# Cross-attention and expert feed-forward: rows of the feed-forward in 32 tiles of 256 and 9 of 128, with three buffers of raw weights

## The chip, the cores and the metric

The kernel runs on one core of one Trainium2 chip. The time is the device time of the whole program in microseconds; the median of three runs of the kernel before is 916.47 us (913.32 to 917.2). The profile is of one execution of its own.

## What is computed

x is (4, 1024, 256), float32. First a cross-attention with 16 heads of 64 over a context of 77 rows is added to x. Then each of the 4096 rows is normalised, scored against 9 experts, and the two best experts of each row are applied and added, weighted:

```
logits = x @ Wr                        # (4096, 9)
topk_w, topk_idx = top_k(softmax(logits), 2);  topk_w /= sum(topk_w)
hidden = silu(x @ Wg[e]) * (x @ Wu[e]) # 256 -> 704, for each expert e
out    = sum over the two experts of cw[t, e] * (hidden @ Wd[e])   # 704 -> 256
```

So 8192 pairs of row and expert go through the feed-forward, spread unevenly over 9 experts. Wg and Wu are 256 x 704 each, Wd is 704 x 256: 2.2 MB for one expert.

## The kernel before

The attention runs first, 32 steps of 128 rows, written out. In it GpSimd scatters each normalised row twice into expert_in in DRAM, once for each of its experts; each expert has a region there. The feed-forward then reads tiles of W = 256 rows that belong to one expert. Each expert's rows are rounded up to whole tiles, so NT is fixed at 40, the most that can be needed; tiles that are not needed are computed on blank rows all the same, and add into a blank part of the result. Three short tables that VectorE works out after the attention (tile_table: expert, first row and weight slot of a tile; fresh: whether its expert differs from the one before) tell which rows and weights a tile takes.

All products of the feed-forward are float32 made of three products of rounded parts: a value is split into "hi" (rounded by ScalarE) and "lo" (the rest, by VectorE), and hi*hi, hi*lo, lo*hi are accumulated (lines 248 to 250). This holds for the weights too: every tile splits its whole expert, six pieces (PIECES: four of 704 columns, one of 1280, one of 256), into wgt_hi and wgt_lo, two buffers of each. The raw weights have two buffers, wgt[0] and wgt[1], by the expert's parity.

One step of the feed-forward, tile j:
- TensorE (expert_step): gate and up products in three units (gate_up, 24, 24 and 18 matmuls of 256 columns; weights stationary, tokens moving, so the hidden rows come out turned as the down product needs them). After the second unit the tokens of tile j + 1 are transposed (tok_turn, line 1183, four transposes), then comes the down product of tile j - 1 (down, lines 248 to 250 and 1216, 34 matmuls), then the third unit.
- ScalarE: silu of a unit, then two pieces of wgt_hi for tile j + 1 (line 930), then the rounding of the hidden rows (946); after the second unit also the tokens of j + 1 (917) and the result of tile j - 1, scaled by the gate (res_move, 957).
- VectorE: the product of a unit (1572 to 1575), two pieces of wgt_lo (1564), the rest of the hidden rows (1583 to 1587); after the second unit the tokens' rest (1552).
- GpSimd: add_results (line 758) scatters the tile's result with addition, two DMAs, waits until they have landed, and then notes gate and row number of tile j + 2 (note, lines 749, 750).
- SyncE (step): waits until tile j - 1 is turned and noted, loads the tokens of tile j + 1 (line 542), loads expert, slot and flag of that tile into registers, and issues its weights (lines 526 to 535), three DMAs for gate and up, three for down, which do nothing where the flag is zero.

The waits that set the order of weight loads and tokens are these:

```python
sp.wait_ge(tok_turned, j)
sp.wait_ge(tok_noted, j)
load_tokens(j + 1, i)
sp.wait_ge(weights_split, j * len(PIECES) - (len(PIECES) - 2 * KT))   # then load_gate_up
sp.wait_ge(weights_split, j * len(PIECES))                            # then load_down
```

Steps 3 to 38 are a loop of two steps (Fori) on every engine; the others are written out. Before step 0 SyncE has loaded the weights of experts 0 and 1 during the end of the attention, blanks the end of each expert's region (store_tail), and loads the tokens of tiles 0 and 1.

## Time and profile before

| | us |
|---|---|
| median of 3 runs | 916.47 |
| profiled execution, its time | 915.46 |
| its span | 913.3 |
| TensorE matmul busy | 848.4 |
| VectorE busy | 694.3 |
| ScalarE busy | 650.1 |
| GpSimd busy | 395.9 |
| raw weights asked for in a tile's step | 3 + 3 DMAs, 40 times |

Times in a timeline are microseconds from the start of the span. A matmul's own duration overlaps that of the next one, so the distance between two starts is what a matmul costs. "x2" on a row is two instructions merged into one row. "SPq" is an instruction that issues a DMA on SyncE. The feed-forward runs from about 389 to the end.

### The profile page before, as it was taken

The numbers are of one execution on the slowest core, as the hardware profiler recorded it, in microseconds if no ns is written. First come the engines' busy times: TensorE is split into PE (matmuls) and PEld (weight loads), VectorE is DVE, ScalarE is ACT, GpSimd is POOL, SyncE is SP. The second block draws the span as 40 slices with busy tenths as digits, with TensorE's granted clock in tenths as the row PEclk, the third lists the DMA queues.
The fourth block names the chain that finished last, engine by engine and source line by source line (L and its number), as shares of the span: only waits on it lengthen the run. The fifth ranks groups of instructions, "written<-read, shape, count | busy, mean of one in ns | idle before, by whom it ended". The sixth has DMA issues, their size and how long they took to land.

```text
span 913.3 us, 21992 instructions
## 1 busy us (share of the span) xinstructions
PE 848.4 (93%) x6494; PEld 810.5 (89%) x6494; DVE 694.3 (76%) x1610; ACT 650.1 (71%) x2009; POOL 395.9 (43%) x536
## 2 busy tenths in 40 slices
PE   6998999999999997099999999999999999999993
PEld 5845999999999996099999999999999999999993
DVE  7577898888898877668777787678687786778771
ACT  3557898898888883267777777677677776777761
POOL 3020387787787676204433333332334333333432
PEclk9999999999999999599999999999999999999997
DMA  8054910400400217602225225444532255222222
GB/s 278 2 148 129 273 37 30 139 31 30 140 31 30 82 37 266 162 25 44 39 46 138 40 46 132 108 102 113 131 47 40 50 133 118 55 41 46 40 29 24
DMA packets 66697, 78.37 MB, mean 86 GB/s; under 512 B 7319, under 2 KB 58707, under 8 KB 66643
## 3 DMA queue, kind: packets, MB, share of 16 engines
q1 hardware_dynamic: 50963, 57.73, 21.5%
q0 software_dynamic: 14592, 18.95, 12.4%
q10 hardware_dynamic: 1088, 1.06, 0.5%
q8 instruction: 24, 0.39, 0.2%
q14 instruction: 30, 0.25, 0.1%
HBM read 113.66 MB, written 33.13 MB: 161 GB/s over the span
## 4 chain that ended last, share of the span: by engine, by line
PE 68%; DMA 12%; issue 7%; SPq 5%; DVE 4%; ACT 2%; POOL 1%; DVEq 0%; ACTq 0%; POOLq 0%
PE banks L248 20%; PE banks L249 19%; PE banks L250 19%; DMA wgt<-in_L_ffn_Wu 5%; PE banks L1116 4%; DMA result<-res,tok_id 3%; DMA valmat_dram<-val_st 2%; PE banks L1216 1%; PE banks L1183 1%; DVE hid_lo L1583 1%; SPq L478 1%; PE banks L1048 1%; POOL result L758 1%; PE banks L1072 1%; PE banks L1084 1%
## 5 line engine op out<-in xcount | busy, mean ns | idle before, releaser
L248 PE MATMUL banks<-tok_t_hi,wgt_hi 128*128 128x256 f32 x880 | 250.6, 285 | 9.7 <-DVE tok_t_lo L1552 9.7
L249 PE MATMUL banks<-tok_t_lo,wgt_hi 128*128 128x256 f32 x880 | 249.6, 284 | 0.0
L250 PE MATMUL banks<-tok_t_hi,wgt_lo 128*128 128x256 f32 x880 | 249.5, 284 | 0.0
L1564 DVE TENSOR_TENSOR wgt_lo<-wgt,wgt_hi 128x704 fp32r<-128x704 f32 (+1 forms) x240 | 207.5, 906 | 38.6 <-ACT wgt_hi L930 37.2
L758 POOL DMA_INDIRECT result<-res,tok_id x80 | 131.2, 1640 | 215.8 <-ACT res L957 188.4
L930 ACT ACTIVATE wgt_hi<-wgt 128x704 fp32r (+3 forms) x240 | 179.8, 800 | 31.2 <-DMA wgt<-in_L_ffn_Wu 24.7
L248 PEld LDWEIGHTS banks<-tok_t_hi,wgt_hi 128*128 128x128 f32 x880 | 169.5, 193 | 11.6 <-issue 11.5
L249 PEld LDWEIGHTS banks<-tok_t_lo,wgt_hi 128*128 128x128 f32 x880 | 169.6, 193 | 0.0
L250 PEld LDWEIGHTS banks<-tok_t_hi,wgt_lo 128*128 128x128 f32 x880 | 169.5, 193 | 0.0
L865 ACT ACTIVATE prob<-banks,row_min 128x77 f32<-128x77 f32 x512 | 161.5, 375 | 4.7 <-DVE row_min L1409 4.7
L865 ACT ACTIVATION_READ_ACCUMULATOR prob<-banks,row_min 128x1 f32 x512 | 131.1, 258 | 0.0
L248 PE MATMUL banks<-wgt_hi,hid_hi 128*128 128x256 f32 x400 | 116.2, 290 | 0.0
L250 PE MATMUL banks<-wgt_hi,hid_lo 128*128 128x256 f32 x400 | 113.1, 283 | 0.0
L249 PE MATMUL banks<-wgt_lo,hid_hi 128*128 128x256 f32 x400 | 113.0, 283 | 0.0
L248 PE MATMUL banks<-valmat_hi,prob_t_hi 128*128 128x266 f32 x320 | 95.1, 297 | 1.7 <-DVE logits L1431 1.7
L710 POOL TENSOR_TENSOR prob<-prob,row_inv 128x1232 f32<-128x1232 f32 x32 | 72.1, 2252 | 56.7 <-DVE row_inv L1423 56.6
L249 PE MATMUL banks<-valmat_lo,prob_t_hi 128*128 128x266 f32 x320 | 92.3, 288 | 0.0
L250 PE MATMUL banks<-valmat_hi,prob_t_lo 128*128 128x266 f32 x320 | 92.2, 288 | 0.0
L749 POOL COPY tok_gate<-tok 128x2 f32<-128x2 f32 x40 | 25.6, 641 | 137.4 <-DMA result<-res,tok_id 124.2
L697 POOL DMA_INDIRECT expert_in<-xn,top_slot x64 | 66.6, 1041 | 38.8 <-POOL xn L687 25.9
L249 PEld LDWEIGHTS banks<-wgt_lo,hid_hi 128*128 128x128 f32 x400 | 76.6, 192 | 0.0
L248 PEld LDWEIGHTS banks<-wgt_hi,hid_hi 128*128 128x128 f32 x400 | 76.6, 191 | 0.0
(197 smaller groups left out, 1983.1 us busy)
## 6 DMA issues: line engine op xcount, KB each, us to landing
wgt<-in_L_ffn_Wg SPq DMA_DIRECT2D x40, 704.0 KB
wgt<-in_L_ffn_Wu SPq DMA_DIRECT2D x40, 640.0 KB
wgt<-in_L_ffn_Wd SPq DMA_DIRECT2D x40, 640.0 KB
tok<-expert_in SPq DMA_DIRECT2D x40, 258.0 KB, 2.8
wgt<-in_L_ffn_Wd SPq DMA_DIRECT2D x80, 64.0 KB
valmat_f<-valmat_dram SPq DMA_DIRECT2D x4, 1197.0 KB, 6.8
expert_in<-blank SPq DMA_DIRECT2D x13, 258.0 KB, 8.3
xs<-in_x SPq DMA_DIRECT2D x3, 1024.0 KB, 12.0
```

What stands on the lines that cost most here:

```text
L248: nc.tensor.matmul(to, a[0], b[0], start=first, stop=False)
L249: nc.tensor.matmul(to, a[0], b[1], start=False, stop=False)
L250: return nc.tensor.matmul(to, a[1], b[0], start=False, stop=last)
L478: sp.dma_start(valmat_dram[b, heads, k:k + r1 - r0, :].rearrange("h k n -> k h n"), staging(n)[r0:r1]).then_inc(val_stored[n % STORE_BUFFE ...
L697: nc.gpsimd.indirect_dma_start(expert_in, bass.IndirectOffsetOnAxis(ap=top_slot[c % 4][:, k:k + 1], axis=0), xn[c % 4][:, k, :], None).the ...
L710: nc.gpsimd.tensor_tensor(p, p, row_inv[i][:].unsqueeze(2).to_broadcast([P, H, M]), ALU.mult).then_inc(prob_ready, 1)
L749: nc.gpsimd.tensor_copy(tok_gate[i][:], tok[i][:, :, GATE])
L758: nc.gpsimd.indirect_dma_start(out, bass.IndirectOffsetOnAxis(ap=tok_id[i][:, a:a + 1], axis=0), res[i][:, a, :], None, compute_op=ALU.add ...
L865: ins = nc.scalar.activation(prob[c % 2][:, h * M:(h + 1) * M], bank[i][:, (h - h0) * M:(h - h0 + 1) * M], ACT.Exp, bias=row_min[c % 2][:, ...
L930: nc.scalar.activation(wgt_hi[i][:, p0:p1], loaded_weights(slot)[:, p0:p1], ACT.Copy).then_inc(weights_hi, 1)
L1116: mm = nc.tensor.transpose(bank[3 + (c * NG + g) % 2][0:n, (m - c0) * P:(m - c0 + 1) * P], prob[c % 2][:, m * P:m * P + n], ident[:])
L1564: nc.vector.tensor_tensor(wgt_lo[i][0:rows, p0:p1], loaded_weights(slot)[0:rows, p0:p1], wgt_hi[i][0:rows, p0:p1].bitcast(F32), ALU.subtra ...
```

## The change

- Rows of an expert are cut into tiles of 256 where at least that much or more than half a tile is there; 32 such tiles in all (NP). What is left over goes into 9 small tiles of 128 rows (NS), whose place in the order is fixed: after the large tiles 3, 6, 10, 13, 17, 20, 24, 27 and 31. So 41 tiles instead of 40, and 9216 rows instead of 10240. A second table (single_table) gives a small tile its expert and first row. VectorE works out this table after the first one, ahead of its first splits of weights.
- In a small tile the tokens are stationary and the weights move (single_gate_up): 512, 512 and 384 columns of gate and up in three banks, two units instead of three. Silu (one operation over 704 columns) and the products are done on rows as they stand, and six transposes (hid_turn) turn the hidden rows for the down product. A small tile splits the weights of the tile after it just as a large one.
- Raw weights of large tiles have three buffers, which the experts take in turn, and a large tile's weights are asked for when the large tile three before has been split. Small tiles have a raw buffer of their own (single_wgt), always loaded, 2.2 MB each, when the small tile before has been split.
- SyncE's step loads the registers once for the gate and up part and once for the down part. At the start it asks for the weights of large tiles 1 and 2, of the first small tile and of large tile 3 before it loads the tokens of tile 2.
- All steps are written out; the loops are gone. Two buffers of hidden rows and one of results lie where the attention's rows (xs) were.
- There are five blank spare tiles to store instead of eight.

The core of the diff (names of buffers and semaphores, table work and the changes of index that follow from it are left out):

```diff
-NT = (2 * B * S + E * (W - 1)) // W
 MAX_TILES = B * S // W
-SPARE = (NT - 2 * B * S // W) * W
+NP = 2 * B * S // W
+NS = 9
+SINGLES_AFTER = (3, 6, 10, 13, 17, 20, 24, 27, 31)
+SEGS = 2 * E
+SPARE = 5 * W
...
+WEIGHT_SLOTS = 3
+
+TILES = []
+for pair in range(NP):
+    TILES.append((WB, pair))
+    if pair in SINGLES_AFTER:
+        TILES.append((1, SINGLES_AFTER.index(pair)))
+NT = len(TILES)
+TILE_UNITS = [UNITS if blocks > 1 else 2 for blocks, _ in TILES]
+UNITS_TO = [sum(TILE_UNITS[:t]) for t in range(NT + 1)]
+SILUS_TO = [sum(UNITS if blocks > 1 else 1 for blocks, _ in TILES[:t]) for t in range(NT + 1)]
+BLOCKS_TO = [sum(blocks for blocks, _ in TILES[:t]) for t in range(NT + 1)]
+PAIR_TILE = [TILES.index((WB, pair)) for pair in range(NP)]
...
+        wgt = sb("wgt", [P, WEIGHT_SLOTS, WCOLS], F32, ffn)
...
+        single_wgt = sb("single_wgt", [P, WCOLS], F32, ffn)
...
+        def weights_loaded(t, gate_up):
+
+            if not is_pair(t):
+                return single_gu_loaded if gate_up else single_d_loaded, (TILES[t][1] + 1) * WEIGHT_LOADS
+            pair = TILES[t][1]
+            loads = pair // WEIGHT_SLOTS + 1 + (pair % WEIGHT_SLOTS == 1)
+            return (wgu_loaded if gate_up else wd_loaded)[pair % WEIGHT_SLOTS], loads * WEIGHT_LOADS
...
+            def pair_place(pair):
+
+                e = sp.value_load(tile_table[0:1, 0, pair:pair + 1], min_val=0, max_val=E - 1)
+                slot = sp.value_load(tile_table[0:1, 2, pair:pair + 1], min_val=0, max_val=WEIGHT_SLOTS - 1)
+                needed = sp.value_load(fresh[0:1, pair:pair + 1], min_val=0, max_val=1) != 0
+                return e, loaded_weights(slot), needed
+
+            def load_pair_gate_up(pair):
+                e, to, needed = pair_place(pair)
+                load_gate_up(e, to, wgu_loaded[pair % WEIGHT_SLOTS], needed)
+
+            def load_pair_down(pair):
+                e, to, needed = pair_place(pair)
+                load_down(e, to, wd_loaded[pair % WEIGHT_SLOTS], needed)
+
+            def load_single_gate_up(k):
+                load_gate_up(sp.value_load(single_table[0:1, 0, k:k + 1], min_val=0, max_val=E - 1), single_wgt[:], single_gu_loaded)
+
+            def load_single_down(k):
+                load_down(sp.value_load(single_table[0:1, 0, k:k + 1], min_val=0, max_val=E - 1), single_wgt[:], single_d_loaded)
...
-            def step(j, i):
-
-                sp.wait_ge(tok_turned, j)
-                sp.sem_inc(loads_begun, 1)
-                sp.wait_ge(tok_noted, j)
-                sp.sem_inc(loads_begun, 1)
-                load_tokens(j + 1, i)
-                e = expert_of(j + 1)
-                slot = sp.value_load(tile_table[0:1, 2, bass.ds(j + 1, 1)], min_val=0, max_val=1)
-                needed = sp.value_load(fresh[0:1, bass.ds(j + 1, 1)], min_val=0, max_val=1) != 0
-
-                sp.wait_ge(weights_split, j * len(PIECES) - (len(PIECES) - 2 * KT))
-                sp.sem_inc(loads_begun, 1)
-                load_gate_up(e, slot, i, needed)
-                sp.wait_ge(weights_split, j * len(PIECES))
-                sp.sem_inc(loads_begun, 1)
-                load_down(e, slot, i, needed)
-
-            for i in range(2):
-                load_tokens(i, i)
...
+            for t in range(2):
+                load_tokens(t)
             sp.wait_ge(fresh_ready, 1)
-            for j in range(1, 3):
-                step(j, (j + 1) % 2)
-            with sp.Fori(0, (NT - 4) // 2) as it:
-                for u in range(2):
-                    step(it * 2 + (3 + u), u)
-
-            sp.wait_ge(added, NT * WB * 16)
+            for pair in range(1, WEIGHT_SLOTS):
+                load_pair_gate_up(pair)
+                load_pair_down(pair)
+            sp.wait_ge(singles_ready, 1)
+            load_single_gate_up(0)
+            load_single_down(0)
+
+            def refill_gate_up(t):
+
+                n = TILES[t][1]
+                if is_pair(t) and n + WEIGHT_SLOTS < NP:
+                    sp.wait_ge(weights_split, t * len(PIECES) + 2 * KT)
+                    load_pair_gate_up(n + WEIGHT_SLOTS)
+                elif not is_pair(t) and n + 1 < NS:
+                    sp.wait_ge(weights_split, t * len(PIECES) + 2 * KT)
+                    load_single_gate_up(n + 1)
+
+            def refill_down(t):
+                n = TILES[t][1]
+                if is_pair(t) and n + WEIGHT_SLOTS < NP:
+                    sp.wait_ge(weights_split, (t + 1) * len(PIECES))
+                    load_pair_down(n + WEIGHT_SLOTS)
+                elif not is_pair(t) and n + 1 < NS:
+                    sp.wait_ge(weights_split, (t + 1) * len(PIECES))
+                    load_single_down(n + 1)
+
+            refill_gate_up(0)
+            for t in range(1, NT):
+                if t + 1 < NT:
+                    sp.wait_ge(tok_turned, t)
+                    sp.wait_ge(tok_noted, t)
+                    load_tokens(t + 1)
+                refill_down(t - 1)
+                refill_gate_up(t)
+
+            sp.wait_ge(added, BLOCKS_TO[NT] * 16)
...
+            for t in range(NT):
+                pool.wait_ge(tok_noted, t + 1)
+                add_results(t)
+                if t + 2 < NT:
+                    note(t + 2)
...
+            def single_step(t):
+
+                last = t == NT - 1
+                src = None if last else weights_of(t + 1)
+                single_silu(t)
+                if not last:
+                    round_pieces(t + 1, 0, src)
+                    tok_move(t + 1)
+                    round_pieces(t + 1, 1, src)
+                res_move(t - 1)
+                single_hid_round(t)
+                if not last:
+                    round_pieces(t + 1, 2, src)
...
+            def single_gate_up(t):
+
+                i = t % 2
+                pe.wait_ge(weights_split, t * len(PIECES) + 2 * KT)
+                pe.wait_ge(tok_split, t + 1)
+                w = [gate_up_of(x) for x in (wgt_hi[i], wgt_lo[i])]
+                for n in range(3):
+                    if n != 1:
+                        unit_free(t, n // 2)
+                    cols = slice(n * 512, min(n * 512 + 512, GU))
+                    to = unit_banks(t, n // 2)[:, n % 2, 0:cols.stop - cols.start]
+                    for k in range(KT):
+                        mm = product(to, [tokens_t(t, part)[:, k, :] for part in range(2)], [x[:, k, cols] for x in w], k == 0, k == KT - 1)
+                    if n:
+                        mm.then_inc(gu_done, 1)
+
+            def hid_turn(t):
+
+                whole, fifth, half = turned_hid(t)
+                pe.wait_ge(hid_made, UNITS_TO[t] + 2)
+                for c in range(FC - 2):
+                    mm = nc.tensor.transpose(whole[:, c, :], single_hid[:, c * P:(c + 1) * P], ident[:])
+                mm.then_inc(hid_turned, 1)
+                nc.tensor.transpose(fifth, single_hid[:, FULL - P:FULL], ident[:])
+                nc.tensor.transpose(half, single_hid[:, FULL:FI], ident[:]).then_inc(hid_turned, 1)
...
+            def single_step(t):
+
+                single_gate_up(t)
+                if t + 1 < NT:
+                    tok_turn(t + 1)
+                down(t - 1)
+                hid_turn(t)
...
+            nc.vector.memset(changed[:, 0:1], 0.0)
+            nc.vector.tensor_tensor(changed[:, 1:NP], expert_f[:, 1:NP], expert_f[:, 0:NP - 1], ALU.not_equal)
+            settle()
+            nc.vector.tensor_tensor_scan(rank[:], ones[:, 0:NP], changed[:], 0.0, ALU.mult, ALU.add)
+            nc.vector.scalar_tensor_tensor(out=fresh[:], in0=expert_f[:], scalar=1.5, in1=changed[:], op0=ALU.is_gt, op1=ALU.mult)
+            settle()
+            for i in range(2):
...
+            def single_step(t):
+
+                last = t == NT - 1
+                src = None if last else weights_of(t + 1)
+                single_hidden(t)
+                if not last:
+                    rest_pieces(t + 1, 0, src)
+                    tok_rest(t + 1)
+                    rest_pieces(t + 1, 1, src)
+                single_hid_rest(t)
+                if not last:
+                    rest_pieces(t + 1, 2, src)
...
```

## Rows read from the trace of the kernel before

**Rows 1.** The page's busy time, share of the span and instructions.

```profile
PE 848.4 (93%) x6494; PEld 810.5 (89%) x6494; DVE 694.3 (76%) x1610; ACT 650.1 (71%) x2009; POOL 395.9 (43%) x536
```

**Rows 2.** Timeline, TensorE: token transposes (start us, us, engine line, operation, operands, count).

```profile
404.44 0.60 PE L1183 MATMUL banks<-ident,tok 128*128 128x128 f32 x4
...
454.16 0.60 PE L1183 MATMUL banks<-ident,tok 128*128 128x128 f32 x4
...
466.60 0.60 PE L1183 MATMUL banks<-ident,tok 128*128 128x128 f32 x4
...
875.74 0.60 PE L1183 MATMUL banks<-ident,tok 128*128 128x128 f32 x4
```

**Rows 3.** Timeline, TensorE: 462 columns in the attention, 256 columns in tile 0.

```profile
221.02 0.37 PE L249 MATMUL banks<-keymat_lo,zn_t_hi 128*128 128x462 f32 x1
221.23 0.37 PE L250 MATMUL banks<-keymat_hi,zn_t_lo 128*128 128x462 f32 x1
...
392.24 0.37 PE L249 MATMUL banks<-tok_t_lo,wgt_hi 128*128 128x256 f32 x1
392.45 0.28 PE L250 MATMUL banks<-tok_t_hi,wgt_lo 128*128 128x256 f32 x1
392.57 0.28 PE L248 MATMUL banks<-tok_t_hi,wgt_hi 128*128 128x256 f32 x1
```

**Rows 4.** Waits, 400 to 900: waiting, releaser, us in total, times, longest.

```profile
ACT wgt_hi L930 <- DMA wgt<-in_L_ffn_Wu: 24.7, 7, 4.2
...
PE banks L248 <- DVE tok_t_lo L1552: 9.7, 7, 2.0
```

**Rows 5.** Timeline, 481 to 496: SyncE, ScalarE, GpSimd where weights are loaded.

```profile
481.56 0.41 SPq L542 DMA_DIRECT2D tok<-expert_in  x1
...
484.43 0.39 SPq L526 DMA_DIRECT2D wgt<-in_L_ffn_Wg  x1
...
492.23 1.48 ACT L930 ACTIVATE wgt_hi<-wgt 128x704 fp32r x2 [2.87 <-DMA wgt<-in_L_ffn_Wu]
...
495.11 0.41 POOL L749 COPY tok_gate<-tok 128x2 f32<-128x2 f32 x1 [6.22 <-DMA result<-res,tok_id]
```

**Rows 6.** Timeline, VectorE, a steady step.

```profile
465.42 0.42 DVE L1587 TENSOR_TENSOR hid_hi<-hid_f,hid_hi 64x256 fp32r<-64x256 f32 x1
...
469.28 1.68 DVE L1564 TENSOR_TENSOR wgt_lo<-wgt,wgt_hi 128x704 fp32r<-128x704 f32 x2
...
471.48 0.68 DVE L1552 TENSOR_TENSOR tok_t_lo<-banks,tok_t_hi 128x512 fp32r<-128x512 f32 x1
```

**Rows 7.** Timeline, ScalarE and GpSimd, from a result to the note.

```profile
471.38 0.84 ACT L957 ACTIVATE res<-banks,tok_gate 128x256 f32<-128x256 f32 x2 [0.88 <-PE banks L1216]
...
478.91 0.91 POOL L749 COPY tok_gate<-tok 128x2 f32<-128x2 f32 x1 [2.46 <-DMA result<-res,tok_id]
```

**Rows 8.** Timeline, SyncE and VectorE, the start of the feed-forward.

```profile
383.88 1.59 SPq L542 DMA_DIRECT2D tok<-expert_in  x2
...
388.72 0.38 SPq L542 DMA_DIRECT2D tok<-expert_in  x1
391.22 0.12 SPq L526 DMA_DIRECT2D wgt<-in_L_ffn_Wg  x1
...
394.44 0.41 SPq L542 DMA_DIRECT2D tok<-expert_in  x1
...
388.49 0.69 DVE L1552 TENSOR_TENSOR tok_t_lo<-banks,tok_t_hi 128x512 fp32r<-128x512 f32 x1 [7.21 <-ACT tok_t_hi L917]
```

**Rows 9.** Windows: busy us of PE, PEld, DVE, ACT, POOL; granted clock; DMA share, GB/s.

```profile
100.00:200.00 100.00, 100.00 (x724) 95.53 (x723) 87.97 (x319) 89.17 (x451) 73.33 (x123) 1.00 0.32 96
384.00:390.00 6.00, 2.90 (x11) 2.13 (x12) 0.75 (x2) 1.28 (x3) 0.68 (x4) 0.50 0.41 94
```

**Rows 10.** Timeline, ScalarE and GpSimd at the end (span 913.3).

```profile
894.78 0.84 ACT L957 ACTIVATE res<-banks,tok_gate 128x256 f32<-128x256 f32 x2 [1.66 <-PE banks L1216]
...
904.87 1.56 POOL L758 DMA_INDIRECT result<-res,tok_id  x1 [0.30 <-issue]
```

531 lines of the change are left out of this document (317 added, 214 removed).

## The prediction

> **What bounds the kernel now.** I read the page's busy shares first: TensorE is busy for 93% of the span, VectorE for 76%, ScalarE for 71% [rows 1]. The change touches only the feed-forward part, so the next view is TensorE's timeline, where the four token transposes of each tile (L1183) make a stamp once a tile. Two neighbouring stamps, 454.16 and 466.60, are 12.44 us apart, others 12.43 [rows 2], and inside such a step the matmuls follow each other without a gap: 256 columns every 0.12 us [rows 3]. 100 matmuls are 12.00 us and the four transposes the other 0.43. So a step is TensorE's own work. From the stamp at 404.44 to that at 875.74 are 37 steps in 471.3 us, and 37 x 12.43 is 459.9: the part loses 11.4 us to something else. The table of waits says what: TensorE waits seven times for the rest of the turned tokens, because ScalarE had waited seven times for an expert's weights [rows 4]. Those are the seven changes to an expert whose weights aren't there yet.
>
> **Fewer columns on TensorE.** 40 tiles of 256 rows become 32 of 256 and 9 of 128. A large tile costs 12.43 us as before. A small one has, with the tokens stationary, six products over 512 + 512 + 384 weight columns, so 12 matmuls of 512 and 6 of 384. The trace has 462 columns every 0.207 us [rows 3]; with 256 in 0.12 that is 0.42 ns a column and 0.0125 us fixed, so 0.2275 and 0.174 us, together 3.77. The down product is 17 x 0.12 = 2.04; two token transposes are 0.21 and six transposes of the hidden rows 0.64 (at 0.107 each, from the 0.43). That is 6.66 us. The sum: 32 x 12.43 + 9 x 6.66 = 457.7 against 40 x 12.43 = 497.2, **-39.5 us**. All of it lies on the path.
>
> The Trainium skill (TensorE: Matmul & The Clock Gate, Back-to-back issue gap) gives about 131 ns for a 512-column matmul in a stream that reloads the array each time, which would make the small gate-up at most 18 x 0.131 = 2.4 us and the sum 12 us lower. The 462-column rows, which also reload each time, stand at 0.207, so the rows speak against that rule and it has no part in the forecast.
>
> **Weight loads earlier.** Weights of a large tile are now asked for three large tiles ahead, into a third buffer, where now the request is made after the tokens of the next tile, in a chain through GpSimd and SyncE: request at 484.43, and ScalarE stands waiting for the data until 492.23 [rows 5]. 30 us ahead covers the 7.7 us of a gate and up load (484.43 to 492.1). All seven waits go: **-11.4 us**. The next thing that is late in those steps is nothing on TensorE; VectorE ends the tokens' rest 1.1 us ahead of the next step (472.16 against 466.60 + 12.43 - 5.76 = 473.27, 5.76 being the 48 matmuls ahead of the stamp) [rows 6].
>
> **What a small tile makes wait.** Each small tile still splits a whole expert for the tile after it, on ScalarE and VectorE, beside half the TensorE work. I walk one: it starts at 0. The down product of the large tile before it is now reached at 3.77 + 0.43 = 4.20, where it used to be reached at 6.2. Its hidden rows are ready when VectorE has finished L1587, which in a step that starts at 466.6 - 5.76 = 460.84 is at 465.84, so at 5.0 [rows 2, 6]: TensorE waits 0.8 us. TensorE then runs to 4.20 + 0.8 + 4.08 + 0.64 = 9.72. VectorE from 5.0: three products for the small tile (about 1.1 by the columns of the 256-column row), four pieces of 704 at 0.80 (half of a 1.69 pair, less the overlap) and the tokens' rest 0.60, to 9.9: another 0.2. The step after it has only 2.04 of down product and is 10.4 us long, against some 9.4 us of VectorE work (76% of 12.43), so nothing is carried on. **+1.0 us x 9 = +9.** Below, the 0.8 could be 0.6; above, with both engines 10% slower than in these rows, the walk gives 2.0 a tile. Bounds +5 and +18.
>
> **Tokens of a tile.** The chain through the queues: ScalarE's result copy at 471.38, GpSimd's two scatters and the waiting for them, its note (from 478.91), SyncE's load at 481.56, 2.8 us to land [rows 5, 7]. From the end of the copy, 472.2, that is 12.2 us, and it serves the transposes of the stamp after next, at 491.5: 7 us to spare. With a small tile between, two steps together are 5 us shorter, less what the copy comes earlier, and some 3.5 us are left. SyncE's own list grows: the expert's row, slot and flag are now loaded twice a tile (for the gate and up part and for the down part), about 8.4 us a tile, still under the shortest distance of 8.7 us between two copies. Where a weight load runs beside the scatters, these land up to 3.7 us later (GpSimd stood 6.22 us before its note where weights were on their way, and 2.46 where none were [rows 5, 7]); nine more such loads come now, one at each small tile. I put **+2.5 us** for them, bounds 0 and +15 (9 x 1.7).
>
> **Start.** Here is the one new wait that I expect to show. SyncE now issues, between the tokens of tile 1 and those of tile 2: both loads for large tiles 1 and 2, the first small tile's two loads, and the first refill. Today a set of three register loads takes from 388.72 + 0.38 to 391.22, 2.1 us, and the six weight issues that follow, none of them needed, plus one more register load reach 394.44 [rows 8]; so a half set (registers, three issues) is about 3.3 us. From 385.5 (the end of the second token load's issue): 4 x 3.3 = 13.2; the small tile 2 x 2.4 = 4.8 (one register load and three real issues each); refill 3.3; register load 0.8. Tokens of tile 2 are asked for at 407.6, land at 410.4 or later, and TensorE wants them at 404.44 [rows 2], with down and gate-up work queued behind that wait. Rounded up for the real load ahead of it in the same queue: **+7 us**, bounds +4 (register loads at 0.6) and +12 (it waits until the small tile's 2.2 MB have gone, at the rate of the 7.7 us load). Such an idle stretch is followed by matmuls at half clock: after the idle time at 386 the granted clock is 0.50 [rows 9] and up to 392.45 the matmuls of 256 columns stand 0.21 us apart [rows 3], 15 of them from 389.2, so **+1.4 us** once more.
>
> The new tables on VectorE add some 25 short operations before the weight split of tile 0, about 5.7 us at 0.17 to 0.3 each. They delay the split of tiles 0 and 1 behind them (eight pieces, 6.6 us), and that work is covered by VectorE's 7.21 us of idle time before 388.49 [rows 8]: 0 us, with 1.5 us of cover left; every microsecond that they take over 7.2 costs one.
>
> **End.** From the last-but-one down product (ScalarE starts on it at 894.78) to the end are 18.5 us: copy, two scatters, their landing, two scatters, the last issued until 906.43, and 6.9 us until 913.3 [rows 10]. The last tile has now one scatter (-1.9), and the small tile's transposes and down product lie beside this chain. With what TensorE does after that point, **-0.5 us**.
>
> Writing the steps out costs or brings 0: the stamps step by the same 12.43 us inside the loop and across its edge, and the attention part, which is written out today, keeps TensorE busy for 100.00 of 100 us [rows 9].
>
> **Sum.** -39.5 - 11.4 + 9 + 2.5 + 7 + 1.4 - 0.5 = -31.5 us. The profiled execution took 915.46 us (span 913.3 and 2.2 around it), 1.0 less than the median of 916.47. 915.46 - 31.5 = 884.0, and 1.0 for the median: **885 us**.
>
> **Rivals.** (a) *Token loads wait behind weight loads.* Both go through SyncE's one queue. If a token load starts only when the weights before it have gone, the start costs 12 instead of 7, and after about half the small tiles the 3.5 us to spare is overrun by some 2 us: 885 + 5 + 9 = 899. For it: a gate and up load took the 7.7 us above with little beside it. Against it: weights come 9 us ahead of tokens and need 7.7. The Trainium skill (DMA: Bandwidth & Descriptors, Two DMAs through the same engine are not ordered) has descriptors of one queue start in order, which is the condition of this rival; no row here shows a token load behind weights. (b) *VectorE and ScalarE bound the small steps more*, at 2.0 us a tile instead of 1.0, and more where the 1.1 us of room is used up: 885 + 9 to 885 + 18, say 897. (c) *The start costs nothing*, because SyncE's register loads don't add up as I take them: 885 - 8.4 = 876.6. (d) *The third buffer doesn't remove the waits for weights*, since another wait on SyncE comes in their place: 885 + 11.4 = 896. (e) *Slower than before*: every small tile lets tokens come late. The place is the transposes two tiles after it. The price is the lateness less 3.5 us; to lose the whole gain it takes 31.5 / 9 = 3.5 us a tile, so tokens 7 us later than now, as they would be if a whole gate and up load (7.7 us) stood in front of each. Fully so at each, with the down part too (another 4 us): 885 + 9 x 4.6 = 926. Against it: the 9 us between the two requests.
>
> **How the numbers follow.** Forecast, 885 with a range of its own of 876 to 893: 0.60. (a) 0.13, (b) 0.08, (c) 0.07, (d) 0.05, (e) 0.04; the rest, 0.03, mixtures that end near 912. The range is 872 (start free, small tiles at their low bound) to 906 (start 12, small tiles 2.0 each). Faster by over 0.5%, about what a measurement of this kernel can tell from no change: 0.94; within: 0.02; slower: 0.04.
>
> **What would show it.** Right: the stamps L1183 12.43 apart between two large tiles, no wait of ScalarE for weights, one wait of TensorE for tokens of 6 to 8 us near 404, nine waits of about 0.8 us ahead of the down product after a small tile's gate-up. Wrong: 512-column matmuls not at 0.2275 us, TensorE waiting for tokens at small tiles, SyncE's third token load before 400, the first matmul of tile 0 later than 389.3.

## The result and the profile after

The kernel after takes 879.12 us (median of 4 executions, 877.32 to 880.56), the kernel before beside it 914.89 (median of 4, 911.4 to 917.2). The ratio is 0.961, with a 95% interval of 0.957 to 0.965. The profiled execution took 879.26 us, its span is 877.5: 35.8 less than the 913.3 of before.

The page's busy time, as in [rows 1], and its line on the DMA packets (78.37 MB in before):

```profile
PE 812.4 (93%) x6049; PEld 767.2 (87%) x6049; DVE 686.9 (78%) x1637; ACT 634.6 (72%) x1980; POOL 367.8 (42%) x531
...
DMA packets 78732, 96.41 MB, mean 110 GB/s; under 512 B 10343, under 2 KB 66083, under 8 KB 78627
```

TensorE has 36 us less to do and is as full as before. 18 MB more are moved.

The token transposes, now L1312 (start us, us, engine line, operation, operands, count), answer to [rows 2]; x2 is the stamp of a small tile:

```profile
385.35 1.12 PE L1312 MATMUL banks<-ident,tok 128*128 128x128 f32 x4 [17.87 <-DMA tok<-expert_in]
...
409.36 0.66 PE L1312 MATMUL banks<-ident,tok 128*128 128x128 f32 x4 [1.98 <-DMA tok<-expert_in]
...
423.33 0.60 PE L1312 MATMUL banks<-ident,tok 128*128 128x128 f32 x4
...
435.76 0.38 PE L1312 MATMUL banks<-ident,tok 128*128 128x128 f32 x2
...
480.86 0.38 PE L1312 MATMUL banks<-ident,tok 128*128 128x128 f32 x2
...
491.13 0.60 PE L1312 MATMUL banks<-ident,tok 128*128 128x128 f32 x4
...
502.97 0.60 PE L1312 MATMUL banks<-ident,tok 128*128 128x128 f32 x4
...
513.54 0.60 PE L1312 MATMUL banks<-ident,tok 128*128 128x128 f32 x4
...
525.96 0.60 PE L1312 MATMUL banks<-ident,tok 128*128 128x128 f32 x4
...
846.32 0.38 PE L1312 MATMUL banks<-ident,tok 128*128 128x128 f32 x2
```

A large tile still takes 12.42 to 12.43 us (513.54 to 525.96). From 480.86 to 513.54 are 32.68 us, two large tiles (24.85) and a small one, so the small one takes 7.83.

Five stretches hold the whole difference. The attention part, up to the stamp of tile 0, ends at 385.35 instead of 386.71: -1.4. From there to the stamp of tile 2 are 24.0 us instead of 17.7: +6.3, and the step behind that stamp takes 13.97 instead of 12.43, +1.5. The rest up to the last stamp (846.32 here, 875.74 before) takes 423.0 instead of 458.9: -35.9. From the last stamp to the end it is 31.2 instead of 37.6: -6.4. Together -35.8 (from the unrounded stamps).

The waits from 400 to 900, as in [rows 4]; all rows of TensorE stand here, and ScalarE has no row of a wait for weights any more:

```profile
PEld banks L311 <- DVE wgt_lo L1789: 7.6, 9, 1.3
...
PE banks L311 <- issue: 6.7, 9, 2.0
...
PEld banks L311 <- issue: 2.6, 2, 2.3
...
PEld banks L1312 <- DMA tok<-expert_in: 2.2, 1, 2.2
...
PE banks L1312 <- DMA tok<-expert_in: 2.0, 1, 2.0
...
PE banks L311 <- DVE wgt_lo L1789: 1.0, 1, 1.0
```

One small tile by the timeline: its gate-up begins at 487.31, each 512 columns of it take 0.23 us and each 384 take 0.18, and its neighbour's down product comes at 492.31 behind an idle gap of 0.58 (by the starts of the matmuls 0.83 are lost there, since 492.31 follows the start before it by 0.85 instead of 0.03 in the run of experiment 2 without backlog):

```profile
487.79 0.40 PE L313 MATMUL banks<-wgt_hi,tok_t_lo 128*128 128x512 f32 x1
...
488.02 0.39 PE L311 MATMUL banks<-wgt_hi,tok_t_hi 128*128 128x512 f32 x1
...
490.77 0.34 PE L312 MATMUL banks<-wgt_lo,tok_t_hi 128*128 128x384 f32 x1
...
490.95 0.34 PE L313 MATMUL banks<-wgt_hi,tok_t_lo 128*128 128x384 f32 x1
...
492.31 0.36 PE L311 MATMUL banks<-wgt_hi,hid_hi 128*128 128x256 f32 x1 [0.58 <-issue]
```

The start of the feed-forward, SyncE, ScalarE and TensorE, beside [rows 8]:

```profile
382.64 1.59 SPq L618 DMA_DIRECT2D tok<-expert_in  x2
...
386.32 0.12 SPq L602 DMA_DIRECT2D wgt<-in_L_ffn_Wg  x1
...
386.88 0.09 SPq L603 DMA_DIRECT2D wgt<-in_L_ffn_Wu  x1
...
387.38 1.47 ACT L1028 ACTIVATE wgt_hi<-wgt 128x704 fp32r x2 [6.41 <-DMA wgt<-in_L_ffn_Wu]
...
388.75 1.06 ACT L1013 ACTIVATE tok_t_hi<-banks 128x512 fp32r<-128x512 f32 x2
...
390.75 0.55 PE L311 MATMUL banks<-tok_t_hi,wgt_hi 128*128 128x256 f32 x1 [2.77 <-DVE tok_t_lo L1773]
...
406.08 0.39 SPq L618 DMA_DIRECT2D tok<-expert_in  x1
```

Here is what I had not foreseen. ScalarE has 6.41 us of waiting for large tile 1's weights. Nothing is loaded for that tile (issues of 0.09 to 0.12 us are those whose condition is false), but the semaphore that ScalarE waits on is raised by these issues too, and SyncE comes to them only behind the two token loads. Behind ScalarE's wait stands the rounding of the turned tokens (388.75), and behind that TensorE's first gate-up matmul: 5.4 us after the stamp of tile 0, where it was 2.6 in before (389.33 against 386.71). The half clock then holds for 29 matmuls (up to 396.87) instead of 15, which is 1.3 us more; in the four other kernels with this start and this late token load it was 14 to 19. The stamp of tile 2 doesn't depend on that: in all five TensorE stands waiting there for the tokens, which SyncE asks for 23.3 to 23.5 us behind the first ones.

### The profile page after: what moved, and what is told of

The parts are those of the page before. It is cut to its first block, busy times and chain, and to the rows that moved or that the text cites. A ratio compares the mean times of both kernels' runs of the same rounds, so it can differ in the third digit from the quotient of the medians.

```text
span 877.5 us, 19817 instructions
## 1 busy us (share of the span) xinstructions
PE 812.4 (93%) x6049; PEld 767.2 (87%) x6049; DVE 686.9 (78%) x1637; ACT 634.6 (72%) x1980; POOL 367.8 (42%) x531
## 3 DMA queue, kind: packets, MB, share of 16 engines
q0 software_dynamic: 13584, 18.03, 11.3%
## 4 chain that ended last, share of the span: by engine, by line
PE 84%; DMA 5%; SPq 4%; DVE 3%; issue 2%; ACT 1%; DVEq 0%; POOL 0%; POOLq 0%; ACTq 0%
PE banks L311 25%; PE banks L312 24%; PE banks L313 24%; PE banks L1241 4%; PE banks L1379 2%; DMA valmat_dram<-val_st 2%; PE banks L1312 2%; PE banks L1173 1%; SPq L554 1%; DMA expert_in<-blank 1%; PE banks L1209 1%; DMA valmat_dram<-late_f 1%; PE banks L1197 1%; PE banks L1224 1%; DMA wkv_sb<-in_L_xattn_Wkv 0%
## 5 line engine op out<-in xcount | busy, mean ns | idle before, releaser
L311 PE MATMUL banks<-tok_t_hi,wgt_hi 128*128 128x256 f32 x704 | 201.9, 287 | 2.9 <-DVE tok_t_lo L1773 2.8
L312 PE MATMUL banks<-tok_t_lo,wgt_hi 128*128 128x256 f32 x704 | 200.3, 285 | 0.0
L313 PE MATMUL banks<-tok_t_hi,wgt_lo 128*128 128x256 f32 x704 | 200.3, 285 | 0.0
L1789 DVE TENSOR_TENSOR wgt_lo<-wgt,wgt_hi 128x704 fp32r<-128x704 f32 (+1 forms) x192 | 165.7, 904 | 19.3 <-ACT wgt_hi L1028 19.1
L1028 ACT ACTIVATE wgt_hi<-wgt 128x704 fp32r (+3 forms) x192 | 143.9, 801 | 18.0 <-DVE wgt_lo L1768 11.1
L311 PEld LDWEIGHTS banks<-tok_t_hi,wgt_hi 128*128 128x128 f32 x704 | 135.8, 193 | 5.2 <-DVE wgt_lo L1789 3.1
L312 PEld LDWEIGHTS banks<-tok_t_lo,wgt_hi 128*128 128x128 f32 x704 | 135.9, 193 | 0.0
L313 PEld LDWEIGHTS banks<-tok_t_hi,wgt_lo 128*128 128x128 f32 x704 | 135.9, 193 | 0.0
L855 POOL COPY tok_gate<-tok 128x2 f32<-128x2 f32 (+1 forms) x41 | 20.5, 499 | 146.1 <-DMA result<-res,tok_id 132.3
L976 ACT ACTIVATE prob_t_hi<-banks 128x512 fp32r<-128x512 f32 (+1 forms) x96 | 48.8, 543 | 35.1 <-PE banks L1241 33.5
```

The source lines that it names most:

```text
L311: nc.tensor.matmul(to, a[0], b[0], start=first, stop=False)
L312: nc.tensor.matmul(to, a[0], b[1], start=False, stop=False)
L313: return nc.tensor.matmul(to, a[1], b[0], start=False, stop=last)
L855: nc.gpsimd.tensor_copy(tok_gate[i][:, 0:blocks], tok[i][:, 0:blocks, GATE])
L976: ins = nc.scalar.activation(prob_t[c % 2][0][0:rows, m0:m1, :], turned_bank(c, g, rows, m0 - c0, m1 - c0), ACT.Copy)
L1028: nc.scalar.activation(wgt_hi[t % 2][:, p0:p1], src[:, p0:p1], ACT.Copy).then_inc(weights_hi, 1)
```

## The experiments

Twelve kernels were run, against the kernel before on the same chip (its medians there: 915.4 to 916.2 us). Stamps are always those of the token transposes. "Less than after" compares with the 879.1 above, which stood beside a before of 914.9; before's own median moves by 1.3 us between these comparisons, so differences of that size are read from the stamps and not from the medians. The diffs are shortened; in the kernels that ask one or two large tiles ahead, large tile 2's loads are also taken out of the start.

**1. The waits for weights in before.** Kernel before, with one number changed:

```diff
-  scalar_tensor_tensor(out=fresh[:, 2:NT], in0=expert_f[:, 2:NT], scalar=1.5, ...
+  scalar_tensor_tensor(out=fresh[:, 2:NT], in0=expert_f[:, 2:NT], scalar=99.0, ...
```

> The kernel before with the flags of new experts all zero from the third tile on: no weights are loaded in the feed-forward after the start (left out: the weights of most experts, so the output differs). Theory A (the seven waits for new experts' weights in before, ScalarE's 24.7 us in all, cost TensorE 11.4 us in all): 11.4 less than before, 903.5. Rival B (the waits cost more than the gaps on TensorE show, by the clock or by VectorE's backlog behind them): 895 to 900. Rival C (the waits were for something else): within 3 us of before.

Measured: 904.1 us, 12.0 less than before. Its stamps:

```profile
406.23 0.60 PE L1183 MATMUL banks<-ident,tok 128*128 128x128 f32 x4
...
866.09 0.60 PE L1183 MATMUL banks<-ident,tok 128*128 128x128 f32 x4
```

459.86 us for 37 steps, where before has 471.30: the waits were 11.44 us, and theory A holds.

**2. Where a small tile's last 1.1 us come from.** Kernel after; first both engines split only 64 columns of each piece, then VectorE alone does:

```diff
                 for n in range(2 * u, 2 * u + 2):
                     p0, p1 = PIECES[n]
+                    p1 = p1 if t < 3 else p0 + 64
```

> The kernel after, where from the fourth tile on ScalarE and VectorE split only 64 columns of each weight piece (left out: the rest of the split weights, so the output differs). TensorE's instructions and the waits stay. Theory A (small tiles are held 1.15 us each by VectorE's splits, large ones by nothing but their columns): a small tile takes 6.66 to 6.9 us and a large one 12.43; 9 x 1.0 = 9 to 10 us less than after, about 870. Rival B (the small tile's extra is TensorE's own, in the change from the gate-up to the down product and the turns): 877 to 879. Rival C (the large tiles too are held by the splits): well under 865.

> The kernel after, where from the fourth tile on VectorE alone writes only 64 columns of each weight piece's rest, and ScalarE rounds in full (left out: most of the rest, so the output differs). Theory A (VectorE's backlog makes a small tile's last 1.1 us): a small tile takes 6.7 to 6.9 us as in the run with both split narrow, 869 to 871. Rival B (ScalarE's chain of rounding and hidden rows makes it): a small tile stays at 7.5 to 7.8 us, 877 to 879. In between: both share it.

Measured: 869.4 us with both narrow and 868.5 with VectorE alone. The stamps of VectorE alone, around the same small tile as above:

```profile
488.28 0.60 PE L1312 MATMUL banks<-ident,tok 128*128 128x128 f32 x4
...
499.21 0.60 PE L1312 MATMUL banks<-ident,tok 128*128 128x128 f32 x4
...
509.59 0.60 PE L1312 MATMUL banks<-ident,tok 128*128 128x128 f32 x4
```

The three steps that hold the small tile (478.03 to 509.59) are 31.56 us, less 24.85 for two large ones: 6.71. So TensorE's own share is 6.71 and VectorE's backlog adds 1.12, all of it; ScalarE's rounding in full adds nothing (with both narrow the three steps are 31.57 us).

**3. Is that backlog a matter of order?** Kernel after; ahead of a small tile the last hidden rows are rounded and their rest taken before the last two weight pieces. On both engines:

```diff
-                    if ahead:
+                    last = ahead and u == UNITS - 1 and not is_pair(t + 1)
+                    if ahead and not last:
                         round_pieces(t + 1, u, src)
                     hid_round(t, u)
+                    if last:
+                        round_pieces(t + 1, u, src)
```

> The kernel after; in the step ahead of a small tile the hidden rows' rounding and rest for the last unit are done ahead of the small tile's last two weight pieces, on ScalarE and VectorE both. Theory A (a small tile's 1.15 us over its 6.66 us of columns is a wait for the hidden rows in the wrong place of the engines' order): the 0.58 us waits ahead of the down product go, 9 x 0.6 = 5 us less than after, 874. Rival B (VectorE has no room in a small step, it is busy without a gap for 8.7 of its 7.81 us and its neighbour's; any order gives the same sum): the wait moves to the next gate-up, within 1 us of after. Rival C (the weight pieces now come late): slower by up to 9 x 0.5 = 4.5 us.

Measured: 882.4 us, 3.3 more than after, as rival C has it. The gap ahead of the down product is gone, and a larger one stands where the weights' rest is now late, at the gate-up behind the small tile:

```profile
499.64 0.39 PE L311 MATMUL banks<-tok_t_hi,wgt_hi 128*128 128x256 f32 x1 [1.42 <-DVE wgt_lo L1792]
```

There are eight of these, 11.3 us in all, and the steps around a small tile are 33.3 us instead of 32.7, so by the stamps the eight cost 5.0 us. VectorE had stood 0.79 us waiting for the hidden rows to be rounded, with no piece to fill that time. The order of after is the better one; what is short is VectorE's time.

**4. The added traffic.** Kernel after, the small tiles' loads after the first replaced by a count:

```diff
-                    load_single_gate_up(n + 1)
+                    sp.sem_inc(single_gu_loaded, WEIGHT_LOADS)
...
-                    load_single_down(n + 1)
+                    sp.sem_inc(single_d_loaded, WEIGHT_LOADS)
```

> The kernel after without the weight loads of the small tiles behind the first one (left out: their own weights, they use those of the first, so the output differs); the waits count on. Theory A (the 18 MB of added traffic costs nothing, it lies beside TensorE's work): within 1 us of after. Rival B (the prediction's term: the added traffic holds tokens and scatters): 2.5 us less than after, 876.6, and up to 15 less at the bound.

Measured: 878.75 us, 0.4 less than after. From the stamp at 423.31 to the last at 846.33 are 423.02 us, and 422.99 in after. 17.8 of the added 18 MB are gone here, and they had cost nothing.

**5. Writing out.** Kernel before, its loop on each of the five engines written out:

```diff
-            with sp.Fori(0, (NT - 4) // 2) as it:
+            for it in range((NT - 4) // 2):
```

> The kernel before, with its loops over pairs of tiles written out on all five engines and nothing else changed. Theory A (writing out costs and gains nothing: a step that crosses the loop's edge is as long as one that does not in before): within 0.3% of before, 912 to 918. Rival B (the loops' branches and their register arithmetic held an engine back): 19 turns of the loop with 0.2 to 0.6 us each, 4 to 11 us less, 903 to 911. Rival C (the fetching of the longer program collides with the transfers): slower by 2 to 10 us.

Measured: 909.7 us (906.0 to 912.2) against 916.2, ratio 0.992 [0.989, 0.995]. My theory (nothing) falls, and rival B is right in the total but not in the place. No step without a wait is shorter. SyncE and ScalarE in the step of [rows 5]:

```profile
480.05 0.41 SPq L542 DMA_DIRECT2D tok<-expert_in  x1
...
482.58 0.39 SPq L526 DMA_DIRECT2D wgt<-in_L_ffn_Wg  x1
...
489.92 1.47 ACT L930 ACTIVATE wgt_hi<-wgt 128x704 fp32r x2 [1.95 <-DMA wgt<-in_L_ffn_Wu]
```

From the stamp ahead of it (477.62 here, 479.02 in before) to the Wg issue it is 4.96 us instead of 5.41, and ScalarE waits 1.95 instead of 2.87 [rows 5]. ScalarE's waits for weights in all fell from 24.7 (seven) to 19.2 (six), TensorE's loss to them from 11.4 to 7.5. But not each of them fell. At three of the seven changes of expert TensorE loses more than in before (1.57, 2.76 and 2.11 us by the stamps instead of 1.32, 2.28 and 1.29), though the request comes earlier there too (ScalarE is ready 5.4 us behind it, and 4.3 to 5.3 us in before): the loads themselves take 7.3 to 10.1 us here from the Wg issue to ScalarE's start, and 7.8 to 9.0 in before. So the earlier request is shown, and that it makes all of the 4.0 is not; what the loads happened to take is in it too. Of the 5.4 us by which the spans differ, another 1.0 lies ahead of tile 0's stamp, which varies that much anyway (below), and 0.4 in the start. In the kernel after, where no expert's weights are waited for in the steady part, the 4.0 are part of the 11.4 and are not gained twice.

**6. When the weights are asked for.** Kernel after, three buffers in all of them. Two large tiles ahead instead of three:

```diff
-                if is_pair(t) and n + WEIGHT_SLOTS < NP:
+                if is_pair(t) and n + 2 < NP:
                     sp.wait_ge(weights_split, t * len(PIECES) + 2 * KT)
-                    load_pair_gate_up(n + WEIGHT_SLOTS)
+                    load_pair_gate_up(n + 2)
```

> The kernel after, where large tile n's step asks for large tile n+2's weights instead of n+3's (two of the three buffers would allow that too: tile n's raw weights are split by then). Theory A (what removed the waits is that the weights are asked for one tile earlier than in before, not the third buffer as such): no wait in the steady part, steps as in after (12.42, and 10.26 + 11.84 + 10.58 around a small tile), within 1 us of after apart from the start, 877 to 880. Rival B (only three tiles ahead is early enough): the waits of before return where no small tile lies between, 1.0 to 2.3 us each at up to seven changes of expert, up to 11 us more, 884 to 890.

Measured: 877.2 us, 1.9 less than after. The steps from the third stamp on are those of after to 0.02 us, without a wait. The 1.9 come from the start: with large tile 2's loads out of it, the tokens of tile 2 are asked for at 400.81 and nobody waits for them. By the stamps the start up to the third one is 4.3 us shorter, and the attention part, which the edit doesn't touch, was 1.2 longer in the profiled execution. So three ahead is no better than two. Two ahead needs only that tile n's raw weights have been split, which two buffers would allow too; that the third buffer can go is argued from this order, and a kernel with two was not built.

One ahead, with the gates and the place of before:

```diff
                     load_tokens(t + 1)
+                    if is_pair(t + 1) and t:
+                        n = TILES[t + 1][1]
+                        sp.wait_ge(weights_split, (t - 1) * len(PIECES) + 2 * KT)
+                        load_pair_gate_up(n)
+                        sp.wait_ge(weights_split, t * len(PIECES))
+                        load_pair_down(n)
```

> The kernel after, where a large tile's weights are asked for in the step ahead of it, behind its tokens, at the gates that before has; the three buffers stay. Theory A (the late request made before's waits): they return at each change of expert, 1.0 to 2.3 us each as in before, more where the step ahead is a small one (7.8 us instead of 12.4 to load in, so up to 4.6 us more); 6 to 9 waits, 10 to 25 us more than after, 889 to 904. Rival B (the third buffer alone removes them): within 2 us of after.

Measured: 912.2 us, 33 more than after, 0.4% less than before: nearly the whole gain is gone, and that is more than theory A had room for. Its waits from 400 to 900, and SyncE and ScalarE in the step of the first large one:

```profile
ACT wgt_hi L1031 <- DMA wgt<-in_L_ffn_Wu: 35.7, 11, 10.4
...
PEld banks L311 <- issue: 33.1, 10, 10.2
...
PE banks L311 <- DVE tok_t_lo L1776: 26.0, 4, 10.0
```

```profile
503.91 0.40 SPq L618 DMA_DIRECT2D tok<-expert_in  x1
...
506.44 0.39 SPq L602 DMA_DIRECT2D wgt<-in_L_ffn_Wg  x1
...
513.40 1.48 ACT L1031 ACTIVATE wgt_hi<-wgt 128x704 fp32r x2 [5.96 <-DMA wgt<-in_L_ffn_Wu]
```

The load takes 7.0 us, no more than in before. But it is asked for 1.0 us ahead of ScalarE's need (513.40 - 5.96 = 507.44), where before asks 4.9 ahead (484.43, and 492.23 - 2.87 = 489.36) [rows 5]. With small tiles between, the token load is 5.7 us behind its stamp instead of 2.5 (498.18 and 479.02 are the stamps), since SyncE issues the small tile's down loads first (501.29 to 503.06). By the stamps, four steps lose 5.5, 5.8, 10.6 and 12.6 us and five lose 0.2 to 0.9: 38 us in all, and the shorter start gives 4.5 back. Of the 3.9 us of lead that are lost at the first large one, 2.9 are a later request (8.3 us behind the stamp instead of 5.4) and 1.1 an earlier need (9.3 instead of 10.3); how much would return without the small tiles' own loads in the queue was not run. In the last two of the four ScalarE is ready 0.5 us behind the request and 1.9 ahead of it (requests at 773.01 and 831.13, ScalarE's starts at 781.86 and 839.59 after waits of 8.30 and 10.37), and the loads take 8.8 and 8.5 us instead of 7.0 and 7.2. Why SyncE is that late there is open. Part of each loss is the clock: behind TensorE's waits of 3.8 and 4.1 us some 16 matmuls stand 0.21 us apart (1.5 us), behind those of 8.2 and 10.0 some 24 (2.2 us).

Large tile n+1 asked for in tile n's step, but only when tile n is split, the down part a step later:

```diff
-                if is_pair(t) and n + WEIGHT_SLOTS < NP:
+                if is_pair(t) and n + 1 < NP and n:
                     sp.wait_ge(weights_split, t * len(PIECES) + 2 * KT)
-                    load_pair_gate_up(n + WEIGHT_SLOTS)
+                    load_pair_gate_up(n + 1)
```

> The kernel after, where large tile n+1's weights are asked for in large tile n's step, instead of three large tiles ahead; the three buffers stay. Theory A (what removed the waits is the early request, which the third buffer allows): the waits for new experts' weights come back on ScalarE, with gaps on TensorE of 1.5 us each where the next tile is a large one of a new expert, up to 11 us more than after, 884 to 890. Rival B (the waits went because the splitting of a small tile lies between, or the loads are issued earlier within the step): within 2 us of after.

Measured: 927.5 us (918.2 to 936.6), 48 more than after and above before. This request is later than that of before (it waits until tile n is split, where before's waits for tile n - 1), which I had overlooked when I wrote theory A. The run says that lateness costs, and the two runs above say how much.

**7. The start.** Kernel after; the tokens of tile 2 asked for behind large tile 1's loads:

```diff
-            for pair in range(1, WEIGHT_SLOTS):
-                load_pair_gate_up(pair)
-                load_pair_down(pair)
+            load_pair_gate_up(1)
+            load_pair_down(1)
+            sp.wait_ge(tok_turned, 1)
+            sp.wait_ge(tok_noted, 1)
+            load_tokens(2)
+            load_pair_gate_up(2)
+            load_pair_down(2)
```

> The kernel after, with one step of SP's order changed: the token load of tile 2 is issued right behind large tile 1's weight loads instead of in tile 1's step. Theory A (the start's second loss is the late token load): turn(2) of TensorE no longer waits (1.98 us <-DMA in after) and the half clock behind it (about 1.4 us lost) does not come; sum 3.4 us less than after, 875.7. The first matmul of tile 0 keeps its distance to turn(0). Rival B (tokens come earlier but tile 2's turn is then held by VectorE's or GpSimd's work at the start): within 1 us of after, 878 to 880. Rival C (weight loads of large tile 2, pushed behind the tokens, are missed): a new wait at tile 2, slower than after by 1 to 3 us.

Measured: 875.9 us, 3.2 less than after. From the stamp of tile 0 to that of tile 2 are 21.7 us instead of 24.0, and the step behind it is 12.42 instead of 13.97, so 3.8 by the stamps. Theory A holds, with the half clock's 1.5 us a loss that doesn't always come (last section).

Then, in addition, large tile 1's loads moved ahead of SyncE's waits for the scatters:

```diff
+            sp.wait_ge(fresh_ready, 1)
+            load_pair_gate_up(1)
+            load_pair_down(1)
             for i in range(4):
                 sp.wait_ge(scattered[i], 32 * (T // 4))
```

> As the run before, and large tile 1's weight loads are issued ahead of SP's waits for the scatter buffers and the blanks, so that ScalarE's rounding for tile 1 finds them done. Theory A (ScalarE's 6.4 us wait for these loads at the start holds back tok_move and thus the first matmul of tile 0): the first gate-up matmul comes back to 1.1 to 2.6 us behind turn(0) (after: 3.88), the half clock ends some 3 us earlier, so 3 to 4 us less than the run with the tokens first alone: 871 to 873. Rival B (the loads are late since the expert's number is late, not since they stand behind the waits): no more than the run with the tokens first, about 875.7.

Measured: 875.2 us, not 871 to 873. The mechanism is right (first gate-up matmul at 389.31, 2.6 us behind the stamp of tile 0, and 18.6 us to that of tile 2), but the stamp of tile 0 comes at 386.69. I took this for the work of the six issues, which now stand ahead of the first tokens: the last ends at 382.90, and the tokens are asked for at 383.89, 8.6 us behind the last issue of blank rows, where it is 6.6 to 8.0 in the other kernels. That makes it likely and doesn't show it, since the stamp of tile 0 varies as much without this edit (see below). So the third version moves only the gate-up loads ahead and puts the down loads behind the first tokens:

```diff
+            sp.wait_ge(fresh_ready, 1)
+            load_pair_gate_up(1)
             for i in range(4):
                 sp.wait_ge(scattered[i], 32 * (T // 4))
...
             for t in range(2):
                 load_tokens(t)
+            load_pair_down(1)
```

> The kernel after with the start mended in two places: large tile 1's gate-up loads stand ahead of SP's waits for the scatters, its down loads behind the tokens of tiles 0 and 1, and the tokens of tile 2 next. Theory A (the run with both loads ahead gave 1.2 us back, since the down loads stood ahead of the first tokens): turn(0) at 385.4 to 386.0, first gate-up matmul 2.6 us behind it, turn(2) 18.6 behind it, 873.5 to 874.5. Rival B (the first tokens' time is set by the scatters, and 386.7 was this run's spread): as that run, 875 to 875.5.

Measured: **873.0 us** (870.4 to 875.2), ratio 0.954 [0.950, 0.958] to before and 6.1 us under after (7.7 by the stamps up to the third one). Its first steps by the timeline:

```profile
384.04 1.11 PE L1316 MATMUL banks<-ident,tok 128*128 128x128 f32 x4 [17.90 <-DMA tok<-expert_in]
...
386.65 0.55 PE L311 MATMUL banks<-tok_t_hi,wgt_hi 128*128 128x256 f32 x1
...
401.92 0.60 PE L1316 MATMUL banks<-ident,tok 128*128 128x128 f32 x4
```

17.9 us from the stamp of tile 0 to that of tile 2, and 17.7 in before: the start costs nothing any more. The stamp of tile 0, at 384.04, is earlier than theory A's 385.4 and than in every other kernel here, so part of this run's time is the attention part's scatter. This is the best version found. Its executions and those of the version ahead overlap (873.6 to 878.2 there), so the 2.2 us between these two are less sure than the 6.1.

## Why the prediction was right, point by point

Predicted were 885 us and -31.5; measured 879.1 and -35.8, inside the forecast's own range.

- **Columns, -39.5.** Right. 512 columns take 0.228 us and 384 take 0.178, where 0.2275 and 0.174 were worked out from 462 and 256 columns; a small tile without backlog is 6.71 us (experiment 2) instead of 6.66, so -39.1. The rule of about 131 ns for 512 columns (the Trainium skill, TensorE: Matmul & The Clock Gate, Back-to-back issue gap) doesn't describe this stream; the rows of before did, to 1 ns at 512 columns and 4 at 384.
- **Waits for weights, -11.4.** The size is right to 0.1 us (experiment 1). The cause was half right: what removes them is when the weights are asked for. Three ahead, which the third buffer was for, does no better than two. And the term is not the worth of the early request in the new kernel: there a request by before's rule costs 33 us (one ahead), mostly since SyncE then comes to it later, behind the small tiles' loads, and less because the need comes earlier.
- **Small tiles, +9.** 9 x 1.12 = +10.1. The walk put 0.8 ahead of the down product and 0.2 ahead of the next gate-up. (Eight of the nine stand between stamps.) Both places are right: by the starts of the matmuls 0.83 are lost at the first (an idle gap of 0.58) and 0.19 at the second, and the three steps lose 1.12 in all. That VectorE is the engine is shown (experiment 2).
- **Tokens and scatters, +2.5.** Wrong, it is 0: no small tile shows a wait for tokens, and taking the added loads away changes nothing (experiment 4). The 3.5 us to spare were enough.
- **Start, +7, and half clock, +1.4.** The sum is right (6.3 + 1.5 = 7.8), and the reason holds, but it was not complete. SyncE's load of tile 2's tokens was put at 407.6; it is at 406.08, with the whole part 1.36 us earlier, so 407.4. But TensorE did not stand 7 us waiting for the tokens, it stood 1.98: it was itself 2.8 us late from the first gate-up matmul and ran at half clock for 1.3 us longer, and both lie inside the time in which the tokens were late. So the late token load sets the 6.3 as forecast. The 1.4 for the half clock came true by luck: in two of the five kernels with this wait no half clock followed (last section). By the experiments, mending the late tokens alone gives 3.8 us, 1.5 of them the half clock, and mending large tile 1's loads, which stand behind the tokens, another 3.8 (24.0 + 1.5 in after, 21.7 with the tokens first, 17.9 with both mended). The second loss, hidden behind the first, I had missed. I had listed "the first matmul later than 389.3" as a sign of a mistake; it was at 390.75.
- **VectorE's tables, 0.** They took 373.67 to 378.8 and put the split of tiles 0 and 1 off by 4.7 us. The weights' rest wasn't what the first matmul waited for [the row at 390.75 names tok_t_lo], so the cover held.
- **Writing out, 0.** Wrong in before, where it gives 6.5 us by the medians (experiment 5; 4.0 of them at the waits for weights, where the loads' own times differ too). I had looked at stamps that hold no wait; the difference sits, at least in part, on SyncE's way to a load that is waited for. In the kernel after it adds nothing that can be seen beside the early requests.
- **End, -0.5.** What is left over: from the stamp of tile 2 on, columns, waits and small tiles make -40.4. The stamps show -42.3 once the half clock's 1.5 us are taken out, so about -1.9. From the result copy of the last-but-one down product to the end are 15.4 us (862.13 to 877.5) instead of 18.5 [rows 10], with one scatter less. No run takes the end apart.
- **The rest of the miss** is the attention part, -1.4, where the change only stores fewer blank rows. It is within the scatter: the stamp of tile 0 was at 385.7 to 387.6 in the three profiled kernels with before's program up to there, and at 385.0 to 387.1 in the nine with after's.
- **Two sums** don't follow from their own terms. The range's upper end, with a start of 12 and small tiles at 2.0, is 885 + 5 + 9 = 899 and not 906. Rival (e) at its worst, 7.7 + 4 - 3.5, is 8.2 us a tile and so 959, not 926. Neither enters the 885.

Of the rivals, (a) would have shown as tokens late at small tiles, (b) as some 2 us a small tile, (c) as a free start, (d) as waits for weights in the steady part, (e) as (a) at every small tile; the rows show none of them.

## What to carry to other kernels

When tiles become shorter, look first at how far ahead of its need each transfer is asked for: here the request one tile ahead, which cost 1.0 to 2.3 us a time before, would have eaten all but 0.4% of a gain of 3.9%. Ask when the data's old place is free, not when the next step begins, and see what else stands in the same queue, which took more of the lead here than the shorter steps did; a conditional load that isn't taken still holds its place there, and whoever waits on its count waits for it. And what an edit such as writing out a loop is worth is read at the steps that wait, not at those that don't.

## What the runs showed of the hardware

- A set of issues whose condition is false is not free: in after SyncE took from 386.32 to 390.47 for large tile 1's six, none of them taken, with the register loads between them.
- An idle stretch of 1.98 us on TensorE, ended at 409.36, was followed by matmuls of 256 columns 0.21 us apart instead of 0.12, beginning 1.2 us after work had started again:

```profile
410.21 0.28 PE L311 MATMUL banks<-wgt_hi,hid_hi 128*128 128x256 f32 x1
...
410.33 0.28 PE L312 MATMUL banks<-wgt_lo,hid_hi 128*128 128x256 f32 x1
...
411.19 0.41 PE L311 MATMUL banks<-wgt_hi,hid_hi 128*128 128x256 f32 x1
...
411.40 0.41 PE L312 MATMUL banks<-wgt_lo,hid_hi 128*128 128x256 f32 x1
```

  A window over it has the granted clock at 0.79, between the levels of 1.2 GHz (0.50) and 2.4 GHz (1.00); gaps of 0.58 us at the small tiles had no such sequel (the clock is 1.00 from 420 to 860). I had expected the half clock here only behind a wait of 7 us.

```profile
408.00:416.00 8.00, 6.64 (x43) 6.64 (x44) 3.73 (x6) 2.87 (x7) 0.00 (x0) 0.79 0.16 43
```

  Whether such a wait costs the clock can't be told from its length here, and that it did in after is partly chance. The same wait for tile 2's tokens was 3.08 us with both splits narrow and 4.23 with the hidden rows first, and the half clock followed; it was 2.63 us without the small loads and 2.70 with VectorE narrow, and none did (granted clock 1.00 in the 6 us behind it, 0.72 in after's). In before, waits of 2.03 and 1.96 us had none either (1.00 from 400 to 900). A wait of 2.0 us in the last down product had none in after (864.77, granted clock 1.00 behind it), and the same one with both splits narrow had (854.37, 0.53). The waits of 3.8 to 10.5 us in the kernels with late requests were all followed by it.

```profile
410.82 0.66 PE L1312 MATMUL banks<-ident,tok 128*128 128x128 f32 x4 [2.63 <-DMA tok<-expert_in]
...
409.11 0.66 PE L1312 MATMUL banks<-ident,tok 128*128 128x128 f32 x4 [2.70 <-DMA tok<-expert_in]
...
602.04 0.38 PE L248 MATMUL banks<-tok_t_hi,wgt_hi 128*128 128x256 f32 x1 [2.03 <-DVE tok_t_lo L1552]
```

  These are from the kernel without small loads, from VectorE narrow and from before.

- SyncE came to a weight load 0.45 us sooner in the written-out kernel than in the loop (4.96 us from a stamp to the Wg issue instead of 5.41, in most steps). Steps without a wait were no shorter for it.
